# Inverse H transform of a 2-D spectral filter: each channel's matmul as two column halves of 64 output rows

## The chip, the cores and the metric

The kernel runs on one core of a Trainium2 chip. The metric is the device time of one launch in microseconds; lower is better. Everything below comes from that core: the run times, one profiled execution, and its trace.

## What is computed

The input `x` is (4, 128, 128, 768) in float32, batch, height, width, channel. The reference, cut to its core:

```python
xf = jnp.fft.rfft2(x, axes=(1, 2), norm='ortho').reshape(b, h, wf, 8, 96)
xr, xi = jnp.real(xf), jnp.imag(xf)
o1r = relu(einsum(xr, w1[0]) - einsum(xi, w1[1]) + b1[0])     # 'bhwni,nio->bhwno'
o1i = relu(einsum(xi, w1[0]) + einsum(xr, w1[1]) + b1[1])
o2r = softshrink(einsum(o1r, w2[0]) - einsum(o1i, w2[1]) + b2[0], 0.01)
o2i = softshrink(einsum(o1i, w2[0]) + einsum(o1r, w2[1]) + b2[1], 0.01)
out = jnp.fft.irfft2((o2r + 1j * o2i).reshape(b, h, wf, c), s=(128, 128), axes=(1, 2), norm='ortho') + x
```

So: a 2-D Fourier transform of each channel, a small complex two-layer network over the channels within each of 8 blocks of 96 channels, and the transform back, plus the input.

## The kernel before

The work is cut into 32 rounds (4 images times 8 channel blocks). A round (`q` in the code) holds one image's 96 channels: 128 x 128 x 96 values, in one of two input buffers `xs[p]`. The main loop runs 16 times over two rounds, p = 0 and p = 1. Within a round TensorE (`pe`) runs these stages one after the other, and every other engine has a queue of its own that follows it by semaphores:

- **Forward lines** (`forward_lines`, L515 and L516): the transform along W. VectorE has folded row pairs of the input beforehand (L878, L880), ScalarE and VectorE pack 4 channels at a time (2 in the last four groups) into one of five ring buffers (L735, L884), and TensorE multiplies. There are 26 groups (`NG`). Per channel there are two matmuls: rows 0 to 63 of the output with the table `fwd_w`, rows 64 to 126 with `fwd_w_odd`. The packed channel is the stationary operand, 64 and 63 of its columns; the table, 128 columns, moves. ScalarE and VectorE move the results out of PSUM (L745, L894).
- **Mixing**: the transform along H (`fwd_big` L549 full array, `fwd_small` L561 in halves of 64 rows, both with the table `fwd_h` moving), the first layer (L574 to L607), the second layer (L624, L633), ReLU on ScalarE (L806), soft shrink on VectorE (L947, L949, L957). VectorE also folds the next round's input in between.
- **Keep warm** (`keep_warm`, L648): five matmuls into a bank nobody reads.
- **Inverse lines** (`inverse_lines`, L528 on TensorE): the transform back along H. This is where the change is. Again 26 groups of 4 or 2 channels in five ring buffers. The packed channel is the stationary operand, 128 columns (one per output row), and the table `inv_h` moves, 128 columns.
- **Rows** (`first_rows`, `rows`; L653 to L655 and L666): the transform back along W. Then VectorE (L966, L973) and GpSimd (L1052, L1058) add the halves and the input, and the sync engine (`sp`) stores the result (L481, L483) and, when all of it is stored, loads the input of the round after the next into the same buffer (L459).

In the inverse lines the order of the work comes from fixed rules. `packer_h(g)` says who fills the ring buffer of group g: ScalarE for groups 0 to 4, 10, 16, 22 (L772 and L739), VectorE for the other odd groups (L888), GpSimd for the other even ones (L1047). The packer of group g waits until TensorE is done with group g - 5, whose ring buffer it takes. The first five groups also wait for a small piece that VectorE packs last (L1013). After each two groups (a unit; there are 13, numbered here 0 to 12) ScalarE copies the head rows out of PSUM (L758) and rounds the rest to `yhi` (L759); VectorE then forms the remainder `ylo` (L907). TensorE's group g uses PSUM bank g mod 8, so from g = 8 on it waits until the unit that holds group g - 8 has been moved (L524). After the last group `first_rows` needs the first ten units for its first part and unit 12 for its second part.

On VectorE one queue holds, unit by unit, the copy that packs an odd group (L888) and then the subtraction L907:

```python
for g in range(NG):
    n = g + RING
    if n < NG and packer_h(n) == "dve":
        pack(q, n)
    if g == UNITS[UNIT_OF[g]][-1]:
        dve.wait_ge(hi_moved, NUNITS * q + UNIT_OF[g] + 1)
        dve.tensor_tensor(taken(ylo), tail, taken(yhi[:, HEAD:H, :]), ALU.subtract)
```

Every float32 matmul of the program appears in the trace as two records of the matmul and two of the weight load: 96 channels in 32 rounds are 3072 matmuls at L528 and 6144 records.

Of the kernel before, what the change touches and what calls it, by code (L numbers as in the profile page):

```python
# [17 lines left out]
HALF = 64  # L18
# [16 lines left out]
RING = 5  # L35
# [6 lines left out]
def packer_h(g):  # L42
    if g < RING or g in (10, 16, 22):
        return "act"
    return "dve" if g % 2 else "pool"
# [6 lines left out]
def upto(owner, g, who):  # L52
    return sum(owner(i) == who for i in range(g + 1))
# [137 lines left out]
def build(nc, x, mix, table, out):  # L191
    with ExitStack() as ctx:
        def sb(name, shape, dt=F32):
            return ctx.enter_context(nc.sbuf_tensor(name, shape, dt))
# [40 lines left out]
        ring = [sb(f"ring{j}", [128, CG, 128]) for j in range(RING)]  # L235
# [5 lines left out]
        ps = ctx.enter_context(nc.psum_tensor("ps", [128, 8, 512], F32))  # L241
# [60 lines left out]
        def mat(name):  # L302
            a, b = COLS[name]
            return tab[:, a:b]
# [19 lines left out]
        def line_bank(stage, g):  # L324

            return (g + ROW0_BANK + 1) % 8 if stage == 0 else g % 8
# [25 lines left out]
        def wait_unit(engine, q, g):  # L352

            engine.wait_ge(head_moved, NUNITS * q + UNIT_OF[g] + 1)
            engine.wait_ge(lo_moved, NUNITS * q + UNIT_OF[g] + 1)
# [91 lines left out]
        with nc.Block() as block:  # L447
# [46 lines left out]
            def _(pe):  # L494
# [24 lines left out]
                def inverse_lines(q):  # L519
                    for g in range(NG):  # L520
                        if g >= 8:
                            wait_unit(pe, q, g - 8)
                        who = packer_h(g)
                        pe.wait_ge(pack_sems[who], PACKED_H[who] * q + upto(packer_h, g, who))  # L524
                        if g < RING:
                            pe.wait_ge(tail_packed, RING * q + g + 1)
                        for j in range(LINE_GROUPS[g][1]):
                            mm = pe.matmul(ps[:, line_bank(1, g), j * 128:(j + 1) * 128], ring[g % RING][:, j, :],  # L528
                                           mat("inv_h"), start=True, stop=True)
                        mm.then_inc(line_done, 1)  # L530

                def lines_moved(q):
# [155 lines left out]
                with pe.Fori(0, STEPS) as t:  # L688
                    for p in range(PAIRS):
# [33 lines left out]
                        mix2_rows(q, NU - 1)  # L723
                        keep_warm(q, 5)
                        inverse_lines(q)
                        first_rows(q)
                        for g in range(1, NF):
# [363 lines left out]
```

## Time and profile before

| | |
|---|---|
| Median of 3 runs | 5081.34 us (5080.94 to 5083.08) |
| The profiled execution, its own time | 5084.92 us |
| Its span, first to last instruction | 5082.8 us |
| TensorE matmul busy | 4944.4 us, 97% |
| TensorE weight load busy | 4268.3 us, 84% |
| VectorE busy | 4024.7 us, 79% |
| ScalarE busy | 2574.7 us, 51% |
| GpSimd busy | 1347.3 us, 27% |
| Mean granted TensorE clock | 0.998 of full speed |
| Share of the last chain | TensorE 81%, VectorE 7%, "issue" 5%, GpSimd 3% |

The profiled execution took 3.6 us longer than the median of the runs, and 2.1 us of its own time lie outside its span. A busy time is the union of the records of an engine, so for matmuls, which overlap one another, it says that some matmul was under way, not how fast they followed each other. The chain is followed back from the last instruction, at each step to what released it.

### The profile page before, as it was taken

What the parts mean: (1) busy time and instruction counts of PE and PEld (TensorE: products, weight loads), DVE (VectorE), ACT (ScalarE), POOL (GpSimd) and SP (SyncE); (2) the same over time, 40 slices, a digit from 0 to 9 for tenths busy, and PEclk for the clock granted to TensorE, in tenths of its full rate; (3) what the DMA queues carried; (4) which work ended last, traced back from release to release, by engine and by line L of the source; (5) the groups of instructions that cost most, each with busy time, mean ns of one, the idle gap of its engine ahead of it and who ended that gap; (6) DMA issues with size and microseconds to landing.
All of it is one profiled execution on the core that took longest, in us unless ns stands there. A gap on an engine that the chain in (4) does not pass through costs nothing.

```text
span 5082.8 us, 113588 instructions
## 1 busy us (share of the span) xinstructions
PE 4944.4 (97%) x43936; PEld 4268.3 (84%) x43936; DVE 4024.7 (79%) x5484; ACT 2574.7 (51%) x3939; POOL 1347.3 (27%) x1285
## 2 busy tenths in 40 slices
PE   7999999999999999999999999999999999999998
PEld 6888888888888888888888888888888888888887
DVE  6878788787787877878778878788787787877876
ACT  4554555545455554555545554555545455454553
POOL 0331123321233312333123331123321233212333
PEclk9999999999999999999999999999999999999999
DMA  3321333312333123331233322333222333123311
GB/s 109 101 72 52 88 101 101 93 45 74 101 101 105 40 66 101 101 105 50 64 94 101 105 60 63 84 101 105 79 58 70 101 105 92 50 66 101 105 51 50
DMA packets 1067734, 420.99 MB, mean 83 GB/s; under 512 B 1064864, under 2 KB 1064992, under 8 KB 1067168
## 3 DMA queue, kind: packets, MB, share of 16 engines
q1 hardware_dynamic: 1062432, 411.63, 29.9%
q8 instruction: 382, 6.26, 0.5%
q10 hardware_dynamic: 4736, 1.60, 0.1%
q14 instruction: 184, 1.51, 0.1%
HBM read 210.26 MB, written 201.33 MB: 81 GB/s over the span
## 4 chain that ended last, share of the span: by engine, by line
PE 81%; DVE 7%; issue 5%; POOL 3%; ACT 2%; DMA 1%; SPq 1%; DVEq 0%; POOLq 0%; ACTq 0%
PE ps L624 13%; PE ps L528 13%; PE ps L549 9%; PE ps L515 7%; PE ps L633 6%; PE ps L561 5%; PE ps L607 4%; PE ps L595 4%; PE ps L653 3%; PE ps L655 2%; PE ps L654 2%; PE ps L574 2%; PE ps L582 2%; PE ps L575 2%; DVE ring L884 2%
## 5 line engine op out<-in xcount | busy, mean ns | idle before, releaser
L1046 POOL TENSOR_TENSOR turn<-turn 1x1 f32<-1x1 f32 x224 | 46.5, 207 | 3499.3 <-PE ps L528 3499.3
L624 PE MATMUL ps<-wts,hbig 128*128 128x192 f32 x4160 | 731.9, 327 | 4.2
L947 DVE TENSOR_TENSOR biased<-ps,wts 128x768 f32<-128x768 f32 (+1 forms) x544 | 501.0, 921 | 266.6 <-PE ps L633 239.8
L515 PE MATMUL ps<-tab,ring 128*64 128x128 f32 x6144 | 692.7, 274 | 9.8 <-ACT ring L735 3.9
L528 PE MATMUL ps<-tab,ring 128*128 128x128 f32 x6144 | 694.6, 276 | 4.2
L528 PEld LDWEIGHTS ps<-tab,ring 128*128 128x128 f32 x6144 | 688.5, 192 | 10.3 <-DVE ring L1013 10.3
L516 PE MATMUL ps<-tab,ring 128*63 128x128 f32 x6144 | 694.3, 274 | 0.0
L515 PEld LDWEIGHTS ps<-tab,ring 128*64 128x64 f32 x6144 | 670.5, 137 | 26.9 <-ACT ydg L745 8.8
L624 PEld LDWEIGHTS ps<-wts,hbig 128*128 128x128 f32 x4160 | 673.0, 190 | 16.4 <-ACT hbig L806 13.7
L516 PEld LDWEIGHTS ps<-tab,ring 128*63 128x63 f32 x6144 | 670.3, 136 | 0.0
L549 PEld LDWEIGHTS ps<-tab,ydg 128*128 128x128 f32 x4032 | 501.3, 191 | 114.1 <-issue 82.9
L549 PE MATMUL ps<-tab,ydg 128*128 128x128 f32 x4032 | 562.3, 282 | 29.4 <-DVE ydg L894 19.1
L783 ACT COPY zbig<-ps 128x512 f32<-128x512 f32 (+1 forms) x544 | 307.3, 568 | 515.8 <-PE ps L549 515.8
L957 DVE TENSOR_TENSOR ydg<-biased,clamped 128x768 f32<-128x768 f32 (+2 forms) x544 | 489.4, 900 | 17.8
L884 DVE COPY ring<-x 128x508 f32<-128x508 f32 (+1 forms) x416 | 404.8, 992 | 118.8 <-PE ps L516 117.6
L907 DVE TENSOR_TENSOR ylo<-ps,yhi 128x864 fp32r<-128x864 f32 (+1 forms) x416 | 403.6, 983 | 92.6 <-ACT yhi L759 91.4
L806 ACT ACTIVATE hbig<-ps,wts 128x1024 f32<-128x1024 f32 (+1 forms) x320 | 305.4, 954 | 327.0 <-PE ps L607 327.0
L925 DVE TENSOR_TENSOR zlo<-zbig,zhi 128x1024 fp32r<-128x1024 f32 (+1 forms) x320 | 326.4, 1020 | 168.5 <-ACT zhi L790 168.5
L797 ACT CAST zsmall_hi<-ps 128x512 fp32r<-128x512 f32 (+1 forms) x320 | 163.1, 510 | 583.8 <-PE ps L561 583.8
L735 ACT COPY ring<-x 128x508 f32<-128x508 f32 (+1 forms) x416 | 440.1, 1095 | 9.5 <-PE ps L516 9.5
L1052 POOL TENSOR_TENSOR x<-ucopy,x 128x480 f32<-128x480 f32 (+1 forms) x288 | 406.6, 1412 | 0.0
L633 PE MATMUL ps<-wts,hsmall 64*128 64x192 f32 x4160 | 401.8, 325 | 0.0
(95 smaller groups left out, 9470.8 us busy)
## 6 DMA issues: line engine op xcount, KB each, us to landing
out<-x SPq DMA_DIRECT2D x352, 480.0 KB, 3.6
x<-in_x SPq DMA_DIRECT2D x192, 768.0 KB, 7.3
x<-in_x SPq DMA_DIRECT2D x32, 816.0 KB, 7.6
x<-in_x SPq DMA_DIRECT2D x32, 720.0 KB, 6.6
out<-x SPq DMA_DIRECT2D x32, 432.0 KB, 4.1
wts<-in_mix SPq DMA_DIRECT2D x16, 513.0 KB, 3.6
out<-x SPq DMA_DIRECT2D x32, 240.0 KB, 3.4
out<-x SPq DMA_DIRECT2D x32, 192.0 KB, 3.6
```

What stands on the lines that cost most here:

```text
L515: pe.matmul(o[0:HALF], slot[:, 0:HALF], mat("fwd_w"), start=True, stop=True)
L516: mm = pe.matmul(o[HALF:127], slot[:, HALF:127], mat("fwd_w_odd"), start=True, stop=True)
L528: mm = pe.matmul(ps[:, line_bank(1, g), j * 128:(j + 1) * 128], ring[g % RING][:, j, :], mat("inv_h"), start=True, stop=True)
L549: mm = pe.matmul(ps[:, z_bank(u, h), k * H:(k + 1) * H], t[:, s:s + 2, :].rearrange("p k c -> p (k c)")[:, 0:BIG], mat("fwd_h"), start=Tru ...
L624: mm = pe.matmul(o, hbig[:, k * H:(k + 1) * H], mix_part("w2_big"), start=first, stop=False, skip_group_check=True)
L633: mm = pe.matmul(o, hsmall[half, pair * H:(pair + 1) * H], mix_part("w2_small")[half], start=False, stop=True, skip_group_check=True)
L735: act.copy(*line_pack_moves(p, g)).then_inc(line_packed_act, 1)
L884: dve.tensor_copy(*line_pack_moves(p, g)).then_inc(line_packed_dve, 1)
L907: dve.tensor_tensor(taken(ylo), tail, taken(yhi[:, HEAD:H, :]), ALU.subtract).then_inc(lo_moved, 1)
L947: dve.tensor_tensor(parts(v), d, b2, ALU.add).then_inc(bias_done, 1)
L957: dve.tensor_tensor(dst, parts(v)[:, :, first:ne, :], parts(c)[:, :, first:ne, :], ALU.subtract).then_inc(shrunk, 1)
L1052: pool.tensor_tensor(xs[p][:, a:b, :], ucopy_of(g), mirror(xs[p], a, b), ALU.add).then_inc(y_plus, 1)
```

## The change

Only `inverse_lines` on TensorE changes. For each channel the one matmul with 128 stationary columns becomes two, with the columns 0 to 63 and 64 to 127 of the packed channel. The first writes PSUM partitions 0 to 63, the second partitions 64 to 127, of the same bank and the same 128 columns. Both have the whole table `inv_h` as their moving operand. The sum over 128 partitions stays whole in both, so each output value is the same sum as before.

```diff
@@ inverse_lines (TensorE)
                         if g < RING:
                             pe.wait_ge(tail_packed, RING * q + g + 1)
                         for j in range(LINE_GROUPS[g][1]):
-                            mm = pe.matmul(ps[:, line_bank(1, g), j * 128:(j + 1) * 128], ring[g % RING][:, j, :],
-                                           mat("inv_h"), start=True, stop=True)
+                            for half in (slice(0, HALF), slice(HALF, 128)):
+                                mm = pe.matmul(ps[half, line_bank(1, g), j * 128:(j + 1) * 128],
+                                               ring[g % RING][:, j, half], mat("inv_h"), start=True, stop=True)
                         mm.then_inc(line_done, 1)
```

In the program's order this touches TensorE alone; `ps<-tab,ring` is the matmul whose stationary operand is the ring buffer and whose moving operand is the table. Before, at the end of the mixing stage and into the inverse lines:

```order
426 L624 MATMUL ps<-wts,hbig 128x192
427 L633 MATMUL ps<-wts,hsmall 128x192
428 L648 MATMUL ps<-tab 128x128 x5
429 L524 ISA
430 L526 ISA
431 L528 MATMUL ps<-tab,ring 128x128 x4
432 L524 REGISTER_ALU
433 L526 REGISTER_ALU
```

and with the change, at the same place (lines behind L528 are numbered one higher):

```order
428 L649 MATMUL ps<-tab 128x128 x5
429 L524 ISA
430 L526 ISA
431 L529 MATMUL ps<-tab,ring 64x128 x8
432 L524 REGISTER_ALU
433 L526 REGISTER_ALU
434 L529 MATMUL ps<-tab,ring 64x128 x8
435 L524 REGISTER_ALU
```

The four matmuls of a group have become eight of half the output rows; nothing else stands between them. The semaphore `line_done` is still raised once per group, by the group's last matmul. The end of the stage before, where TensorE goes on to the rows:

```order
465 L528 MATMUL ps<-tab,ring 128x128 x2
466 L524 REGISTER_ALU
467 L528 MATMUL ps<-tab,ring 128x128 x2
468 L524 REGISTER_ALU
469 L528 MATMUL ps<-tab,ring 128x128 x4
470 L653 MATMUL ps<-yhi,odd_lo 128x4x80
```

With the change these are `x4`, `x4` and `x8` of 64x128, and the full-array matmul of the first row follows directly, as before. VectorE, ScalarE, GpSimd and the sync engine have the same instructions in the same order (825, 584, 146 and 142 rows in both).

## Rows read from the trace of the kernel before

**Rows 1.** The page: engines over the span, and the costliest TensorE groups, busy us, mean ns.

```profile
span 5082.8 us, 113588 instructions
PE 4944.4 (97%) x43936; PEld 4268.3 (84%) x43936; DVE 4024.7 (79%) x5484; ACT 2574.7 (51%) x3939; POOL 1347.3 (27%) x1285
...
L528 PE MATMUL ps<-tab,ring 128*128 128x128 f32 x6144 | 694.6, 276 | 4.2
...
L528 PEld LDWEIGHTS ps<-tab,ring 128*128 128x128 f32 x6144 | 688.5, 192 | 10.3 <-DVE ring L1013 10.3
...
L515 PEld LDWEIGHTS ps<-tab,ring 128*64 128x64 f32 x6144 | 670.5, 137 | 26.9 <-ACT ydg L745 8.8 <-issue 6.9 <-ACT ring L735 4.7
```

**Rows 2.** Inverse lines of one round in order of time, TensorE: start us, us, count.

```profile
621.00 1.38 PE L648 MATMUL ps<-tab 128*128 128x128 f32 x10
622.51 21.70 PE L528 MATMUL ps<-tab,ring 128*128 128x128 f32 x192
```

**Rows 3.** The same stage by narrower windows, and its weight loads.

```profile
622.51 0.71 PE L528 MATMUL ps<-tab,ring 128*128 128x128 f32 x4
...
624.73 18.48 PE L528 MATMUL ps<-tab,ring 128*128 128x128 f32 x164
...
624.85 18.28 PEld L528 LDWEIGHTS ps<-tab,ring 128*128 128x128 f32 x163
```

**Rows 4.** Forward lines of the next round in order of time, TensorE.

```profile
664.21 0.32 PE L515 MATMUL ps<-tab,ring 128*64 128x128 f32 x1
664.22 0.32 PE L516 MATMUL ps<-tab,ring 128*63 128x128 f32 x1
664.37 0.27 PE L515 MATMUL ps<-tab,ring 128*64 128x128 f32 x1
...
669.28 0.27 PE L515 MATMUL ps<-tab,ring 128*64 128x128 f32 x1
```

**Rows 5.** Mixing stage in order of time, TensorE: full array, halves, full array.

```profile
687.75 0.61 PE L549 MATMUL ps<-tab,ydg 128*128 128x128 f32 x4
688.29 1.09 PE L561 MATMUL ps<-tab,ydg 128*64 128x128 f32 x16
689.32 0.49 PE L549 MATMUL ps<-tab,yedge 128*128 128x128 f32 x2
```

**Rows 6.** Chain that ended last, end of the inverse lines of that round: start, us, what.

```profile
642.44 0.02 issue
642.46 0.04 ACT ydg L758
642.51 0.15 issue
642.65 0.89 ACT yhi L759
```

**Rows 7.** VectorE in order of time; in brackets the idle time before and its releaser.

```profile
635.73 1.06 DVE L907 TENSOR_TENSOR ylo<-ps,yhi 128x864 fp32r<-128x864 f32 x1 [0.53 <-ACT yhi L759]
...
642.86 0.40 DVE L888 COPY ring<-ydg 128x256 f32<-128x256 f32 x1
643.57 2.09 DVE L907 TENSOR_TENSOR ylo<-ps,yhi 128x864 fp32r<-128x864 f32 x3 [0.31 <-ACT yhi L759]
```

**Rows 8.** VectorE between 635.73 and 643.26 us: length, busy us, count.

```profile
635.73:643.26 7.53, 7.47 (x10) 1.00 0.01 2
```

**Rows 9.** ScalarE in order of time, around group 16 and at the stage's end.

```profile
633.53 1.20 ACT L739 COPY ring<-ydg 128x512 f32<-128x512 f32 x1 [0.71 <-PE ps L528]
...
644.37 0.53 ACT L759 CAST yhi<-ps 128x432 fp32r<-128x432 f32 x1
```

**Rows 10.** TensorE in order of time, into the rows of that round.

```profile
643.97 0.40 PE L653 MATMUL ps<-yhi,odd_lo 128*128 128x320 f32 x1
...
644.50 0.83 PE L666 MATMUL ps<-ydg,tab 128*128 128x400 f32 x2
645.80 0.27 PE L653 MATMUL ps<-yhi,odd_lo 128*128 128x64 f32 x1 [0.47 <-DVE ylo L907]
```

**Rows 11.** Waits, whole span: us in total, times, longest us.

```profile
DVE x L878 <- DMA x<-in_x: 63.7, 28, 7.1
...
PE ps L499 <- DVE ucopy L973: 18.8, 15, 1.3
PE ps L653 <- DVE ylo L907: 15.1, 32, 0.5
```

## The prediction

> **What bounds the kernel now.** I read the page first. TensorE has a matmul under way for 97% of the span and the next engine is at 79% [rows 1], so the question is how fast TensorE's matmuls follow one another, which a busy share does not tell. The changed matmuls, L528, have 6144 records and 694.6 us of busy time, 13.7% of the span. Each record lasts 276 ns while the group's busy time per record is 113 ns: they overlap, and what counts is the time from start to start.
>
> So next I read one round in order of time. Its inverse lines take 21.70 us for 192 records, without a break [rows 2]. In the steady part 164 records fill 18.48 us; without the last one's own 0.275 us that is 18.205 / 163 = **111.7 ns from start to start**, and the weight loads have the same step, (18.28 - 0.192) / 162 = 111.7 [rows 3]. The first step is longer: the first four records take 0.71 us, which leaves 0.71 - 0.275 - 2 x 0.1117 = 0.21 us for it.
>
> TensorE is not waiting for packers or PSUM in this stage, so it sets its end. The chain confirms it: TensorE finishes unit 10 (176 records) at 642.44, ScalarE starts at once, rounds `yhi` from 642.65 for 0.89 us [rows 6], VectorE does its last three subtractions back to back from 643.57 for 2.09 us [rows 7], and TensorE, idle for 0.47 us, starts the second part of the first row at 645.80 [rows 10]. That wait comes once in each of the 32 rounds, 15.1 us in all [rows 11].
>
> **What the change costs and gives.** It takes away 6144 records of full width and puts in 12288 of half width, as 6144 pairs.
>
> *Pace of a pair.* The forward lines already run this shape: two matmuls with 64 and 63 stationary columns, into the lower and the upper partitions of one bank. They start 0.01 us apart, at 664.21 and 664.22, and run beside each other [rows 4]. From 664.37 to 669.28 there are 45 steps of the pair: 4.91 / 45 = **109.1 ns**. There the two halves have different moving tables; in the change both read the same one. L561 is nearer in this: halves with the same moving table. Its 16 records, 8 pairs, take 1.09 us [rows 5]; without the last one's 0.27 and a first step of 0.16, six steps remain for 0.66 us, 0.11 each, the same within what two decimals allow. I take 109.1 ns. A pair is thus 2.6 ns shorter than the full-width record, though it does the same work.
>
> The bounds of the pace: the forward lines from below, 109.1; from above no gain at all, 111.7, if the short run of L561 hides 2.6 ns; and far above, two halves one after the other, 218.
>
> The Trainium skill, "TensorE: Matmul & The Clock Gate", section LDWEIGHTS, puts a weight load at its columns divided by 1.2 GHz: by that page an estimate of 107 ns for the full width and 53 for a half. Both lie below the steps of 111.7 and 109.1, so by the page alone no load would hold up a matmul, the pace would not change and the sum would be near zero; that is the second rival below. The rows of L528 and L515 decide otherwise, and so do their loads of 192 and 137 ns [rows 1], which are longer than the page's.
>
> *First step.* A pair's first step is 664.37 - 664.21 = 0.16 us [rows 4], against 0.21 now: 0.05 us gained per round.
>
> *Gain of the stage.* At the end of unit 10, which is what the chain follows: 0.05 + 174 x 2.6 ns = 0.50 us. At the last record: 0.05 + 190 x 2.6 ns = 0.54 us.
>
> *Changing the array's shape.* At L549 to L561 and back the rows show the price [rows 5]. L549's last record starts 0.275 before its end, at 688.09; L561 begins at 688.29, 0.20 us later instead of 0.11. Back again, L561's last starts at 689.11 and L549 at 689.32, 0.21 later, and L549's first step is 0.49 - 0.275 = 0.21 instead of 0.11. That is some 0.1 us into the halves and 0.2 us out of them. The way in costs nothing: keep-warm ends 622.38, and TensorE stands idle until the packed data at 622.51 [rows 2]. The way out is covered by the wait for `ylo`: now the first part begins at 643.97 and its last matmul ends at 645.33 [rows 10]. After the change the last pair starts at about 643.40, the first part at 643.61, and it ends at about 645.0. The second part's release, 0.50 us earlier, comes at 645.30. So 0.3 us of cover is left. Should it be gone, the cost is at most 0.3 us a round.
>
> The Trainium skill's "TensorEngine Tiling (Array Packing)", section Key Properties, says that changing the tiling mode drains TensorE. Taken as fully exposed, twice a round, it would leave about 5 to 6 us of gain, by the prices of [rows 5]; by the rows both changes fall into idle time.
>
> *Can the others keep up?* VectorE is the tight one. Between 635.73 and 643.26 it is busy for 7.47 of 7.53 us [rows 8]. That stretch starts after ScalarE's copy at 633.53, which TensorE released when group 11 was done, 96 records in [rows 9]. By then the gain is 0.05 + 94 x 2.6 ns = 0.29 us, so VectorE could be free for unit 10 at 643.26 - 0.29 = 642.97. The data for it, `yhi`, come 0.50 us earlier than 643.54, at 643.04. VectorE is ready 0.07 us before them, and the whole 0.50 us passes through.
>
> VectorE also packs group 25, now ready at 642.86 + 0.40 = 643.26, then at 642.97. TensorE wants it at 622.67 + 187 x 0.1091 = 643.07, and its weight load about 0.1 us sooner. A stall of up to 0.1 us can appear there. It touches only the last records, whose `yhi` is ready at 644.90 [rows 9] while VectorE comes to it near 645.1 (three subtractions in 2.09 us, the last two of half size), so the chain is not moved.
>
> *Later stages.* Everything behind the stage starts from it: rows, VectorE's and GpSimd's additions, the stores, the loads that wait for the stores, and the folds. VectorE does wait for loaded input, 63.7 us in 28 waits, and TensorE for VectorE before the forward lines, 18.8 us [rows 11]. But a load is issued when the stores of the same rows are done, so these waits move with the stage and keep their length. No transfer and no queue goes around the inverse lines. I cost this at nothing.
>
> Sum: 32 x 0.50 = **16 us**. The profiled execution would go from 5084.9 to 5068.9; the median of the runs lay 3.6 us below it, and from that median, 5081.3, I forecast **5065.3 us**.
>
> **Rivals.**
>
> *VectorE ends the stage.* If its copies and subtractions stretch by more than the 0.07 us of room, the gain is what reached the start of its busy stretch: 0.29 us a round, 9.3 us, giving 5072. For it: the room is a seventh of the gain, and three engines take turns with five ring buffers. Against: the gain at VectorE's start is worked out from one round, and an earlier TensorE makes none of VectorE's instructions longer. A mixture with half of the 0.3 us of the shape's changes exposed on top keeps 0.14 us a round, 4.5 us: 5077.
>
> *No gain in pace.* If the 109.1 ns need different moving tables or output of 63 rows, the pair steps at 111.7 and only first steps and drains change: 5080 to 5083. L561 speaks against it.
>
> *Slower: the halves run one after the other.* At a step of 218 ns instead of 111.7, the stage grows by 192 x 0.106 = 20.4 us a round, 650 us in all, giving 5734. The place is the pair at L529; the point from which it decides is a step above 111.7 + 2.6 = 114.3 ns, where the loss is as large as the forecast gain. For it: both halves now read the same stationary buffer and the same table at once, and twice as many instructions pass TensorE's queue. Against: the forward lines issue the same four instructions per step, two loads and two matmuls, and read both halves of the same ring buffer [rows 4]; L561 shares its table [rows 5]. Only both together are new.
>
> **How the numbers follow.** About 0.2%, 10 us, is what a measurement of this kernel can tell from no change. Forecast, 14 to 18 us gained: 0.66. VectorE or the drain takes a part, 4 to 13 us gained: 0.20, a third of it above 10 us. No gain in pace: 0.09. Slower: 0.05. So faster by over 0.2%: 0.66 + 0.06 = 0.72; within: 0.23; slower: 0.05. The range goes from 5063 (18 us, the whole 0.54 us and a little) to 5077 (the weakest mixture); it leaves out the last two rivals.
>
> **What would show it.** In the changed profile each L529 pair starts within 0.01 us and steps by 109 ns; the stage takes 21.70 - 0.54 = 21.16 us, or up to 0.1 more with a wait at group 25. ScalarE is released for unit 10 0.50 us sooner after the stage's start, and the wait for `ylo` shrinks from 0.47 to about 0.3 us but stays. TensorE's weight loads at L529 take 137 instead of 192 ns each. A step of 111.7 ns, or a wait of VectorE before unit 10 that has vanished while TensorE's wait for `ylo` grew, would tell that the forecast is wrong, by the first or the second rival; a step of 218 ns would tell the third.

## Result and the profile after

The changed kernel takes 5100.5 us (median of 6 runs, 5094.9 to 5107.9), the kernel before 5082.2 us (6 runs, 5080.9 to 5088.4). The ratio is 1.0032, with a 95% interval of 1.0020 to 1.0044: **slower by 0.3%**, where 16 us less were forecast.

The changed stage did what was forecast. In order of time, TensorE in the changed kernel (start us, us, count; in brackets the idle time before):

```profile
471.00 1.38 PE L649 MATMUL ps<-tab 128*128 128x128 f32 x10
472.52 21.18 PE L529 MATMUL ps<-tab,ring 128*64 128x128 f32 x384
493.63 0.42 PE L654 MATMUL ps<-yhi,odd_lo 128*128 128x320 f32 x1
...
495.34 0.27 PE L654 MATMUL ps<-yhi,odd_lo 128*128 128x64 f32 x1 [0.32 <-DVE ylo L908]
```

The inverse lines take 21.18 us instead of the 21.70 of [rows 2], and the wait for `ylo` has shrunk from the 0.47 us of [rows 10] to 0.32. The whole way from the start of the inverse lines to the start of the second part is 495.34 - 472.52 = 22.82 us, before it was 645.80 - 622.51 = 23.29: 0.47 us gained, in each of the 32 rounds. Yet the page of the profile says (span; queues of DMA with packets, MB, share of the 16 engines' time):

```profile
span 5096.8 us, 125876 instructions
...
q1 hardware_dynamic: 1062432, 411.63, 29.9%
q8 instruction: 430, 7.05, 0.6%
```

The span is 14.0 us longer than in [rows 1]. One queue has changed: `q8 instruction`, which brings the engines' own instructions. It was 382 packets and 6.26 MB before, 16 KB each; now it is 48 more. TensorE has 12288 records more, 6144 of matmuls and 6144 of weight loads; 0.79 MB over 12288 are 64 bytes for each.

The waits of the changed kernel over the whole span (us in total, times, longest us):

```profile
DVE x L879 <- DMA x<-in_x: 77.4, 30, 7.6
...
PE ps L550 <- DVE zsmall_lo L929: 30.5, 24, 3.2
```

VectorE waits 13.7 us more for loaded input than in [rows 11], and TensorE waits 30.5 us in the mixing stage for a result of VectorE, `zsmall_lo`, that stands behind the folds in VectorE's queue. For comparison, the kernel before:

```profile
PE ps L549 <- DVE zsmall_lo L928: 10.3, 19, 1.9
```

Adding up the 31 complete rounds of both traces stage by stage gives the account (from first and last start of a stage's records):

| us over the launch | before | changed | difference |
|---|---|---|---|
| start of inverse lines to end of rows, 32 rounds | 1281.4 | 1266.4 | -15.0 |
| forward lines, 31 | 675.0 | 676.3 | +1.3 |
| mixing, 31 | 2879.4 | 2905.7 | +26.3 |
| first inverse lines begin at | 152.6 | 153.9 | +1.3 |

So the 15 us came, and 26 us were lost in a stage that the diff does not touch: 19.8 of them in the 16 mixing stages that follow an even round (p = 0), 6.5 in the 15 others.

**One round in detail.** Round 2, whose inverse lines start at 466.68 us before and at 472.52 after. GpSimd's last result is ready 60.4 us after that start before, and 59.9 after; the gain has reached it. The last two stores follow, and the DMA view of the 3.3 us around them (packets, MB, share of 16 engines; issues with us to landing) reads, before, from 526.7 to 530.0 us:

```profile
q1 hardware_dynamic: 2673, 1.01, 117.5%
issues: line engine op xcount, KB each, median us to landing
out<-x SPq DMA_DIRECT2D x1, 240.0 KB, 3.4
out<-x SPq DMA_DIRECT2D x1, 192.0 KB, 3.6
```

and in the changed kernel, from 532.0 to 535.3 us, nearly the same place in its round:

```profile
q1 hardware_dynamic: 2433, 0.92, 107.9%
q8 instruction: 1, 0.02, 1.8%
issues: line engine op xcount, KB each, median us to landing
out<-x SPq DMA_DIRECT2D x1, 240.0 KB, 3.6
out<-x SPq DMA_DIRECT2D x1, 192.0 KB, 5.0
```

One packet of instructions lies among the stores; it starts at 532.6 us, as the last two stores are issued, and the last store lands after 5.0 instead of 3.6 us. The kernel before is not free of such packets. A wider window, from 524.4 to 533.1 us, shows one too:

```profile
q8 instruction: 1, 0.02, 0.9%
```

It starts at 530.3 us, 63.6 us after the start of the inverse lines, in the last 1.1 us of the store, which still lands after 3.6 us. So what counts is when a packet comes, and not whether one does.

All loads of the next input are issued behind the last landing: the first one 65.1 us after the start of the inverse lines before, and 66.1 us after it with the change. VectorE's folds in the round, changed kernel:

```profile
545.92 1.06 DVE L879 TENSOR_TENSOR x<-x 128x864 f32<-128x864 f32 x1 [1.84 <-DMA x<-in_x]
...
552.33 1.16 DVE L879 TENSOR_TENSOR x<-x 128x960 f32<-128x960 f32 x1 [4.26 <-DMA x<-in_x]
...
558.00 0.68 DVE L929 TENSOR_TENSOR zsmall_lo<-ps,zsmall_hi 128x512 fp32r<-128x512 f32 x1
```

and before:

```profile
538.62 1.05 DVE L878 TENSOR_TENSOR x<-x 128x864 f32<-128x864 f32 x1
...
543.74 1.16 DVE L878 TENSOR_TENSOR x<-x 128x960 f32<-128x960 f32 x1 [2.98 <-DMA x<-in_x]
...
549.40 0.69 DVE L928 TENSOR_TENSOR zsmall_lo<-ps,zsmall_hi 128x512 fp32r<-128x512 f32 x1
```

Counted from the start of the inverse lines, the second fold begins at 77.1 us before and at 79.8 after, and `zsmall_lo`, for which TensorE waits, at 82.7 and 85.5. Of these 2.7 us the late stores account for 1.0. The second fold waits for the fourth load; it is issued at 69.5 us before and at 70.9 us after, and it takes longer. Before (issued between 536.0 and 536.4 us):

```profile
x<-in_x SPq DMA_DIRECT2D x1, 768.0 KB, 7.5
```

and changed (between 543.3 and 543.6 us):

```profile
x<-in_x SPq DMA_DIRECT2D x1, 768.0 KB, 8.8
```

In the changed kernel a second packet of instructions starts at 77.5 us, while this load is under way; before, the next one starts at 81.0, behind it. How much of the 1.3 us longer transfer that second packet makes, no run separates.

TensorE at that place, the kernel before:

```profile
550.24 1.16 PE L549 MATMUL ps<-tab,ydg 128*128 128x128 f32 x8
```

and the changed one:

```profile
558.74 2.07 PE L550 MATMUL ps<-tab,ydg 128*128 128x128 f32 x8 [3.06 <-DVE zsmall_lo L929]
```

TensorE idles for 3.06 us, and its clock falls. Windows of the changed kernel (busy us and count of TensorE, its weight loads and the others; granted clock; DMA share; GB/s), ahead of the fall and in it:

```profile
550.00:557.00 7.00, 5.67 (x52) 4.21 (x51) 4.60 (x5) 3.09 (x4) 0.00 (x0) 1.00 1.03 278
...
557.80:564.60 6.80, 5.86 (x18) 5.00 (x19) 6.56 (x9) 0.59 (x1) 0.00 (x0) 0.50 0.53 145
```

For 6.8 us it runs at the lower of its two levels, 1.2 GHz. The mixing stage in which all of this lies takes 98.3 us; the same one before took 92.5. In the changed kernel the clock is at 0.50 in such stretches for 13.6 us in all, between the first round and the tail; before, in none. An estimate from these numbers: the waits for `zsmall_lo` grew by 30.5 - 10.3 = 20.2 us, and half of 13.6 us is 6.8 at most for the clock, together 27 us, about the 26.3 that mixing lost.

### The profile page after: what moved, and what is told of

Its sections match the earlier page's. It is cut to its first block, busy times and chain, and to the rows that moved or that the text cites. A ratio compares the mean times of both kernels' runs of the same rounds, so it can differ in the third digit from the quotient of the medians.

```text
span 5096.8 us, 125876 instructions
## 1 busy us (share of the span) xinstructions
PE 4939.2 (97%) x50080; PEld 4257.0 (84%) x50080; DVE 4021.5 (79%) x5484; ACT 2573.4 (50%) x3939; POOL 1353.1 (27%) x1285
## 4 chain that ended last, share of the span: by engine, by line
PE 79%; DVE 7%; issue 5%; POOL 5%; ACT 2%; DMA 2%; SPq 1%; DVEq 0%; POOLq 0%; ACTq 0%
PE ps L625 13%; PE ps L529 12%; PE ps L550 9%; PE ps L634 6%; PE ps L515 6%; PE ps L562 5%; PE ps L608 4%; PE ps L596 4%; PE ps L575 2%; PE ps L654 2%; PE ps L656 2%; POOL x L1053 2%; POOL x L1059 2%; PE ps L655 2%; PE ps L583 2%
## 5 line engine op out<-in xcount | busy, mean ns | idle before, releaser
L515 PE MATMUL ps<-tab,ring 128*64 128x128 f32 x6144 | 691.8, 274 | 12.0 <-DVE ring L885 6.7
L515 PEld LDWEIGHTS ps<-tab,ring 128*64 128x64 f32 x6144 | 670.6, 137 | 28.3 <-ACT ydg L746 9.6
L625 PEld LDWEIGHTS ps<-wts,hbig 128*128 128x128 f32 x4160 | 672.8, 190 | 16.4 <-ACT hbig L807 13.7
L529 PE MATMUL ps<-tab,ring 128*64 128x128 f32 x12288 | 677.9, 273 | 4.2
L529 PEld LDWEIGHTS ps<-tab,ring 128*64 128x64 f32 x12288 | 670.1, 137 | 10.4 <-DVE ring L1014 10.3
L550 PE MATMUL ps<-tab,ydg 128*128 128x128 f32 x4032 | 564.4, 283 | 49.6 <-DVE zsmall_lo L929 30.5
L908 DVE TENSOR_TENSOR ylo<-ps,yhi 128x864 fp32r<-128x864 f32 (+1 forms) x416 | 403.3, 982 | 82.7 <-ACT yhi L760 82.7
```

Source lines behind the costliest of these rows:

```text
L515: pe.matmul(o[0:HALF], slot[:, 0:HALF], mat("fwd_w"), start=True, stop=True)
L529: mm = pe.matmul(ps[half, line_bank(1, g), j * 128:(j + 1) * 128], ring[g % RING][:, j, half], mat("inv_h"), start=True, stop=True)
L550: mm = pe.matmul(ps[:, z_bank(u, h), k * H:(k + 1) * H], t[:, s:s + 2, :].rearrange("p k c -> p (k c)")[:, 0:BIG], mat("fwd_h"), start=Tru ...
L625: mm = pe.matmul(o, hbig[:, k * H:(k + 1) * H], mix_part("w2_big"), start=first, stop=False, skip_group_check=True)
```

## The experiments

Two theories stood against each other. **A**: the changed kernel brings more instructions over the DMA engines, and brings them at other moments; where such a fetch meets the last stores of a round or the first loads behind them, these land late, and VectorE and TensorE follow. **B**: the halves themselves cost something outside their stage.

**Cut the path from the stores to the folds.** Each quarter of the next input gets loaded once the rows that it overwrites are stored, instead of after all stores of the round. `LOAD_AT` is `{2: (0,), 4: (1,), 5: (2,), 6: (3,)}`: behind the third batch of stores the first quarter, and so on; each quarter has a semaphore of its own.

```diff
-                        for g in STORE_AFTER:
+                        for k, g in enumerate(STORE_AFTER):
...
+                            for i in LOAD_AT.get(k, ()):
+                                sp.wait_ge(stored[p][i], (t + 1) * 32 * PIECE_OF.count(i))
+                                if not last:
+                                    load_x((q + PAIRS) // B, (q + PAIRS) % B, p, [i])
-                        sp.wait_ge(stored[p], (t + 1) * 16 * STORES)
-                        if not last:
-                            load_x((q + PAIRS) // B, (q + PAIRS) % B, p)
```

With the halves:

> The changed kernel, and each quarter of the next input is loaded as soon as the rows that it overwrites are stored, instead of after all stores of the round. Theory A (the stores and loads land later because more TensorE instructions are fetched over the same DMA engines, at other moments, and the loads hang on the last store): the wait of VectorE for loaded input (77 us in 30 waits) nearly vanishes, the 26 us that the mixing stages grew go, and the time is about 5060 us, 15 us below the whole-matmul kernel with the same loads. Theory B (the halves themselves cost time outside their stage, for instance by slowing other engines): it stays at 5080 to 5100 us, above the whole-matmul kernel with the same loads.

With whole matmuls:

> The kernel before with the same early loads. Theory A: its mixing stages lose the 13 us by which they exceed 92.45 us a round, so about 5069 us; the kernel with halves is 12 to 17 us below it. Theory B: the kernel with halves is above it by some 15 us, as the change was above the kernel before.

Measured: 5055.8 us with the halves (ratio to the kernel before 0.9946, 0.9932 to 0.9959) and 5071.9 us with whole matmuls (0.9979, 0.9970 to 0.9988). The distance is **16.2 us**, the forecast's 16. In both traces the mixing stages add up to the same 2867.5 us. The waits with the halves and early loads:

```profile
DVE x L883 <- DMA x<-in_x: 12.9, 4, 7.3
...
PE ps L658 <- DVE ylo L912: 10.3, 32, 0.3
```

With the loads off the path the halves are worth what their stage says. B, taken as a cost of the halves outside their stage whatever the loads do, falls here. The halves with early loads are the fastest of all: 26.8 us below the kernel before, measured together.

**Move the fetches from within the loop.** 14 matmuls more in each round, which are 28 records of matmuls and 28 of weight loads, by cutting the 512 moving columns of `mix1_columns` (L595) in two:

```diff
-                    for i in range(halves(u)):
+                    step = n // 2 if n == 4 * H else n
+                    for a in range(0, n, step):
+                        for i in range(halves(u)):
...
```

> The kernel before (inverse lines as whole matmuls) with the 512 moving columns of the mix1_columns matmuls cut in two: 56 more TensorE instructions a round at about 5 ns each, 1 to 2 us in all by themselves. It moves where the blocks of instructions are fetched without touching the inverse lines. Theory A: the landing of the stores and the time change by more than that, 3 us or more in either direction. Theory B: 5083 us, up to 2 us above the kernel before.

> The changed kernel with the same cut in mix1_columns. Theory A: the time moves by 3 us or more against the changed kernel's 5100 us, in either direction, since the fetches fall elsewhere. Theory B: 5101 to 5102 us.

The "56 more" in the first counts records of matmuls and loads together. Its "5 ns each" is no measured figure and does not give its "1 to 2 us" (56 x 32 x 5 ns are 9 us); where no fetch disturbs it, a mixing stage of this kernel takes 0.04 us more than before, 1.3 us in all. Measured: 5083.7 us with whole matmuls (1.0003, 0.9993 to 1.0012), **a miss for A**, which wanted 3 us or more; and 5110.4 us with the halves (1.0053, 1.0038 to 1.0069), 10 us above the changed kernel, as A wanted. By themselves these two left open that the halves are what makes a kernel sensitive.

**Move the fetches without touching the loop.** The program is fetched in 16 KB blocks, which at the 64 bytes from above are 256 instructions. Matmuls that run once, while TensorE waits for the first input, shift the loop against the blocks; 16 of them are 64 instructions, a quarter of a block. The edit, with n = 16, 32 or 48:

```diff
                 pe.wait_ge(cleared, 1)
+                for i in range(n):
+                    pe.matmul(ps[:, Z_BANK, 0:H], mat("fwd_w"), mat("fwd_w_odd"), start=True, stop=True)
```

> The changed kernel with 16 matmuls more (64 TensorE instructions, a quarter of a 16 KB fetch) once, before the main loop, while TensorE waits for the first input anyway. Nothing in the loop changes. Theory A (what costs the time is where the fetches of TensorE's instructions fall against the last stores and first loads of a round): if fetches are cut at fixed places of the program, each falls a quarter of a fetch elsewhere, and the time moves by 5 us or more from 5100 us, in either direction; in the profile a round is slow where a fetch falls within the last stores or the first load. Theory B (the halves in the loop cost it by themselves, wherever fetches fall): 5098 to 5101 us.

> The same with 32 matmuls (half a fetch). Theory A: another time again, 5 us or more from 5100 us or from the one with 16, in either direction. Theory B: 5098 to 5101 us.

> The same with 48 matmuls (three quarters of a fetch). Theory A: of the four places of the fetches (0, 16, 32, 48) at least one gives 5090 us or less. Theory B: 5098 to 5101 us.

> The kernel before with 32 matmuls ahead of the loop. Theory A: its fetches, of which none falls between 65 and 77 us after the start of an even round's inverse lines, move by half of one, into the last stores or the first load; slower than before by 4 us or more. Theory B: within 2 us of the kernel before.

> The kernel before with 16 matmuls ahead of the loop. Theory A (places of the fetches decide): another time than 5082 us by 4 us or more, in either direction. Theory B, as it is left after the first eight runs (the places matter for the kernel with halves; the whole-matmul kernel was only hit in one unlucky case): within 3 us of 5082 us.

> The kernel before with 48 matmuls ahead of the loop. It is compared with the halves and 48 first, 5071.7 us. Theory A: the change is worth its 16 us on the mean over the four places (0, 16, 32, 48): the halves' mean is 5093.7 us, so the whole matmuls' mean is near 5110 us, with 5082.5 and 5136.8 us known. Theory B: 5082 us, and the means do not differ by 16 us.

Measured, medians in us with the ratio to the kernel before and its interval:

| matmuls ahead of the loop | whole | halves |
|---|---|---|
| 0 | 5082.2 | 5100.5, 1.0032 (1.0020 to 1.0044) |
| 16 | 5084.8, 1.0001 (0.9992 to 1.0011) | 5099.3, 1.0033 (1.0021 to 1.0045) |
| 32 | 5136.8, 1.0103 (1.0086 to 1.0120) | 5103.5, 1.0034 (1.0022 to 1.0047) |
| 48 | 5117.3, 1.0067 (1.0051 to 1.0084) | 5071.7, 0.9977 (0.9967 to 0.9987) |
| mean of the four | 5105.3 | 5093.7 |

The loop is the same in each column. Yet the whole-matmul kernel spans 55 us and the halves 32 us, and with 48 matmuls ahead the halves beat the kernel before by 11.7 us, measured together. (The kernel before itself had medians of 5082.2 to 5084.9 us at the different times of measuring, so times of different rows can be compared to within some 3 us.) Three of the six single expectations failed: 16 ahead moved neither kernel by the 4 or 5 us that A asked for, and 32 ahead moved the halves by 3 us only. A holds as to the mechanism, but it cannot say beforehand by how much a shift moves the time. The mean over the four places favours the halves by 11.5 us; 16 were expected, and four places are few.

What ties place and time together is a count over the even rounds (p = 0) of the ten kernels that load at the end, 160 rounds. Each is sorted by whether a packet of the instruction queue of 16 KB starts between 57.5 and 62.5 us after the start of the inverse lines (the last stores), or between 68 and 74.5 us (the first loads):

| fetch at the last stores | fetch at the first loads | rounds | last landing after GpSimd's last result | mixing, mean |
|---|---|---|---|---|
| no | no | 87 | 4.4 us | 92.8 us |
| no | yes | 16 | 4.9 us | 94.2 us |
| yes | no | 13 | 5.7 us | 95.0 us |
| yes | yes | 44 | 5.4 us | 95.1 us |

Where neither happens, mixing takes 92.8 us with whole matmuls (50 rounds) and 92.8 with halves (37). The kernel before has none of its 16 even rounds hit, the changed kernel 11, and the halves with 48 ahead again none.

Taken by kernel the count is sharper. Five have no even round hit, with whole matmuls (the kernel before, 16 ahead, and more instructions) or with halves (32 and 48 ahead): their mixing stages add up to 2876.5 to 2888.4 us. The other five have 11 to 16 hit, again with whole matmuls (32 and 48 ahead) or with halves (none and 16 ahead, and more instructions): 2905.7 to 2923.5 us. With the loads as they are, the place of the fetches sorts the kernels, and halves or whole matmuls do not.

Three things limit this count. The two windows were drawn after the rounds had been seen. Five of the 87 rounds that are not hit (two with whole matmuls and more instructions, three with halves and 32 ahead) have a packet at 64.1 to 64.6 us; their last store lands 5.8 or 5.9 us after GpSimd's last result, and mixing takes 94.4 to 96.1 us. In the kernel before, three rounds with a packet at 64.4 or 64.5 us have landings of 4.5 us, and yet mixing of 93.7 to 94.5. So the first window is not the only bad place. And in the odd rounds of the kernel before a packet starts at 71.9 to 73.5 us each time, within the second window, while mixing takes 92.5 to 93.1 us: a fetch at the first loads alone is not always dear.

The store window of round 2 in the kernel with halves and 48 ahead, from 523.6 to 526.9 us, has no packet of `q8` in it, and the last store lands as it did before the change:

```profile
q1 hardware_dynamic: 2653, 1.00, 116.3%
issues: line engine op xcount, KB each, median us to landing
out<-x SPq DMA_DIRECT2D x1, 240.0 KB, 3.4
out<-x SPq DMA_DIRECT2D x1, 192.0 KB, 3.6
```

**A second cost of the place.** With 32 ahead, whole or halves, a wait appears in the forward lines that no other kernel has at this size. Whole matmuls, 32 ahead:

```profile
PE ps L515 <- issue: 30.0, 15, 2.3
```

Halves, 32 ahead:

```profile
PE ps L515 <- issue: 29.5, 15, 2.5
```

In order of time, one of the fifteen in the whole-matmul kernel:

```profile
985.38 0.46 PE L499 MATMUL ps<-x,tab 128*128 128x96 f32 x2 [1.26 <-DVE ucopy L975]
...
989.19 0.27 PE L515 MATMUL ps<-tab,ring 128*64 128x128 f32 x1 [1.79 <-issue]
```

The main loop jumps back fifteen times, and each time TensorE stops about 2 us, some dozen channel steps behind the jump. Nothing in the views of waits releases it. The queue `q8` does tell something: in each of the fifteen stalls, in all four kernels that have 32 matmuls ahead, one packet of 16 KB starts 2.2 to 2.7 us before TensorE goes on. The other kernels nearly always have a packet in the same place, 0.8 to 1.8 us after the start of the forward lines of an even round, and no stall. And 32 ahead costs about one packet more per turn of the loop, 398 instead of 382 with whole matmuls and 446 instead of 430 with halves, though 32 matmuls are only half a block. So TensorE waiting for its own instructions is the reading that fits. That the packet is TensorE's the trace does not tell.

**Both together.**

> Halves, early loads, and 32 matmuls ahead of the loop, the place that was worst for the whole matmuls. Theory A: late stores and loads no longer reach the mixing stage (2867 us in all, as with early loads before), so of the cost of this place only TensorE's stall behind the jump back of the loop is left, 2 us in each of 15 iterations, 28 to 30 us: about 5085 us. If the place reached the time mainly through the loads, 5056 to 5060 us.

> Whole matmuls, early loads, 32 matmuls ahead of the loop. Theory A: 5100 us, the stall of 28 to 30 us added to 5072 us, and 14 to 17 us above the halves at the same place. If halves themselves cost time where fetches collide, the distance is under 8 us.

Measured: 5094.2 us (1.0008, 0.9997 to 1.0019) and 5114.4 us (1.0058, 1.0041 to 1.0074). The waits of the first at the stall:

```profile
PE ps L519 <- issue: 31.0, 15, 2.3
```

The stall is there, 31 us, and the halves stay below, by 20 us. Three of the ten runs of the first took 5083.1 to 5085.4 us, as was expected, and the other seven 5093.3 to 5096.9. By the medians the two are 9 and 14 us slower than expected: mixing is 2875.5 and 2873.9 us instead of 2867.5, and the clock falls to 0.50 in some rounds, for 13.6 us with the halves and 23.9 with whole matmuls, which the expectation left out. Early loads thus take away most of the first cost and none of the second.

## Why the prediction was wrong

**What bounds the kernel; pace of a pair; first step.** Right. The step from the forward lines and L561, 109.1 ns, was the one to take: 384 records in 21.18 us against 21.16 forecast. The rival without gain in pace is out, and so is that of halves one after the other.

**Gain of the stage: right, 0.47 us measured against 0.50.** Over 32 rounds that is 15.0 us against the sum's 16. VectorE held nothing back, so that rival did not come, and no wait at group 25 appeared.

**Changing the array's shape: right.** The way out of the halves is covered; the second part still waits 0.32 us. The drain that the Trainium skill names ("TensorEngine Tiling (Array Packing)", Key Properties) cost nothing here. By the prices of [rows 5] a full exposure would have left 16 - 32 x 0.3 = 6.4 us of gain, not the "5 to 6" of the text; and the 5734 us of the slower rival start from the profiled execution, from the median they would be 5731.

**Later stages: wrong, and this is the step that failed.** The text said that all waits "move with the stage and keep their length", that "no transfer and no queue goes around the inverse lines", and costed it at nothing. One transfer does: the fetch of the engine's own instructions. It follows the place of the loop in the program: shifts that leave every store and semaphore as they are moved the packets and the time. The text also had the link between stores and loads too loose. It said that "a load is issued when the stores of the same rows are done", but in this kernel every load waits for all stores of its round, so one late store delays all eight loads. The change put 768 more instructions into each turn of the loop, three blocks, and set the others at other moments. The cost was 26.3 us of mixing. Doubled instructions were mentioned under the slower rival only as a load on TensorE's queue; their way over the DMA engines was not looked at, though the page of the profile names the queue and its packets.

The Trainium skill gives the size of a block: "Advanced Engine Details and Errata", section ISA Cache, has 16 KB, 256 instructions. The traces agree: 6.26 MB in 382 packets, and 48 packets more for 12288 instructions. What it says of the number of such blocks that an engine holds no run here shows.

**The rest of the chain** was read, but its slack was not. [rows 11] held 63.7 us of waits for loaded input and I let them pass as moving along. What counted was that the second fold had no room: before, even rounds with a fold at 76.9 to 77.2 us had 92.5 us of mixing, and the few at 78.3 to 79.0 already 93.7 to 94.5. A store that takes 1.4 us longer thus reaches TensorE, and in round 2 it arrived there as 2.8 us, because the loads behind it took longer too.

## What to carry to other kernels

A change that raises an engine's instruction count also moves the moments at which its code is fetched; if a transfer with no slack hangs on "all stores done", a fetch of 16 KB among them can cost more than the change gains. Before judging a change of a few tenths of a per cent in a long unrolled loop, shift the loop by a few dozen instructions in both versions and compare over several places, or first take the fragile transfer off the path. Here the loads by quarters did that, and with them the change was worth its full 16 us.

## What the runs showed that I had not expected

- The place of the loop against the 16 KB blocks alone is worth up to 53 us, 1.0%: 5083.4 to 5136.8 us, measured together, with the same loop. Some 30 us of them are the stall behind the jump. The kernel before happened to sit at a good place, level with 16 ahead and 32 to 53 us better than the two others.
- One packet of instructions, about 1 us long in the records (0.9 to 1.9), went with a store that landed 1.4 us later, 5.0 instead of 3.6 us. While these stores run, the packets take over 100% of the 16 engines' time, and the kernel goes on only when all 16 signals of a store have come, so one held-up engine would be enough. That is an argument; which engine carried the fetch the trace does not tell.
- Three times in the changed kernel the granted clock went from 1.00 to 0.50, for 3.4 or 6.8 us, each time beside a wait of TensorE in the mixing stage, of 3.2, 3.1 and 2.1 us. Other waits, of up to 2.4 us, left it at 1.00, so the length of the wait alone does not decide. Such stretches add up to 30.7 us where mixing was longest, in the halves with 14 matmuls more a round.
- A record of a full-width float32 matmul with 128 moving columns steps at 111.7 ns, and the pair of halves side by side that replaces it at 109.1 ns: the same work in twice the instructions is 2.3% faster in its own stage.
